# A cleared piece of unused memory behind each row scatter of a routed mixture of experts

## What is computed

```python
x = _layernorm(x + _L0_attn_ref(x, ...))             # gated delta-rule attention, 6 heads
x = _layernorm(x + _L0_xattn_ref(x, ctx, ctx, ...))  # causal softmax attention, 16 heads, 4 of keys
x = _layernorm(x + _L0_ffn_ref(x, ...))              # mixture of experts

# _L0_ffn_ref: 16 routed experts, 2 chosen per token, and 2 shared ones
aff = sigmoid(einsum('bsd,de->bse', x, wa))
topk_p, topk_i = top_k(aff, 2)
topk_p = topk_p / sum(topk_p, axis=-1, keepdims=True)
combine = sum(one_hot(topk_i, 16) * topk_p[..., None], axis=2)
routed = einsum('bsed,bse->bsd', experts_all(x, rg, rgb, rw1, rb1, rw2, rb2), combine)
shared = sum(experts_all(x, sg, sgb, sw1, sb1, sw2, sb2), axis=2)
return x + shared + routed
# an expert: w2(gelu(x g + gb) * (x w1 + b1)) + b2
```

## Time and profile before

| | us |
|---|---|
| median of 3 runs | 576.19 (575.22 to 576.56) |
| the profiled execution | 576.92 |
| its span, first to last instruction | 575.1 |
| TensorE busy | 472.9 (82%) |
| VectorE busy | 364.8 (63%) |
| ScalarE busy | 259.8 (45%) |
| GpSimd busy | 240.9 (42%) |
| L2209, 32 scatters | 31.4 busy, 25.0 idle before them |
| L2231, 48 scatters | 46.2 busy, 61.5 idle before them |

### The profile page before, as it was taken

The page is one execution under the profiler, slowest core; times in us unless marked ns, Lnnn a source line. Parts: engine busy times, 40 slices in busy tenths (PEclk is TensorE's granted clock), DMA queues, the critical chain, the costliest instruction groups (busy, mean ns, idle before and its releaser), DMA issues.

```text
span 575.1 us, 15459 instructions
## 1 busy us (share of the span) xinstructions
PE 472.9 (82%) x5644; PEld 342.5 (60%) x5644; DVE 364.8 (63%) x870; ACT 259.8 (45%) x657; POOL 240.9 (42%) x303
## 2 busy tenths in 40 slices
PE   4969889478769899999689999828983779999765
PEld 2434344244559899997467777614541568888554
DVE  0759468479957566667568799805641067777536
ACT  2557565535663344455366767502100034444316
POOL 0328021246016675643655544170373026555600
PEclk9989999789799999999799999978997979999968
DMA  8980000017662732003660000030053815554284
GB/s 289 284 252 1 0 0 0 2 47 241 237 124 51 181 109 54 22 3 75 249 253 2 3 2 4 6 113 1 30 195 126 284 39 178 163 171 132 84 301 146
DMA packets 62019, 64.00 MB, mean 111 GB/s; under 512 B 31412, under 2 KB 51964, under 8 KB 61564
## 3 DMA queue, kind: packets, MB, share of 16 engines
q1 hardware_dynamic: 58108, 52.29, 29.4%
q0 software_dynamic: 3840, 10.75, 5.2%
HBM read 37.01 MB, written 28.25 MB: 113 GB/s over the span
## 4 chain that ended last, share of the span: by engine, by line
PE 48%; DVE 25%; issue 12%; ACT 5%; SPq 5%; DMA 4%; POOL 1%; DVEq 0%; POOLq 0%; ACTq 0%
PE ps L1161 7%; DVE work L1593 5%; PE ps L732 5%; PE ps L954 4%; DVE work L1772 3%; DVE arena L1776 3%; PE ps L1178 3%; PE ps L722 3%; SPq L675 3%; PE ps L935 2%; PE ps L1083 2%; ACT arena L1440 2%; PE ps L908 2%; PE ps L920 2%; PE ps L886 2%
## 5 line engine op out<-in xcount | busy, mean ns | idle before, releaser
L1593 DVE SCALAR_TENSOR_TENSOR work<-ps,colp,work 96x504 f32<-96x504 f32 (+5 forms) x84 | 59.6, 729 | 21.9 <-ACT work L1235 19.9
L2231 POOL DMA_INDIRECT rows_dr<-work,dest_i x48 | 46.2, 962 | 61.5 <-DVE work L2009 31.2
L1161 PE MATMUL ps<-vsg,work 128*128 x192 | 51.5, 392 | 0.4 <-ACT work L1524 0.4
L732 PE MATMUL ps<-xT,front 128*96 128x512 f32 (+3 forms) x112 | 50.5, 595 | 0.0
L2209 POOL DMA_INDIRECT slots_dr<-xn,slots_i x32 | 31.4, 982 | 25.0 <-issue 9.2
L722 PE MATMUL ps<-front,work 128*128 128x396 f32 x64 | 26.7, 568 | 15.3 <-ACT ab L1228 8.2
L2151 POOL TENSOR_TENSOR arena<-front,consts 128x384 f32<-128x384 f32 x32 | 26.5, 832 | 29.4 <-DMA front<-inverse_dr 24.0
L1530 ACT ACTIVATE work<-work 128x128 f32<-128x128 f32 x48 | 14.8, 309 | 53.0 <-DVE work L1994 43.4
L1994 DVE TENSOR_TENSOR work<-ps,xT 128x256 f32<-128x256 f32 x48 | 20.4, 425 | 28.1 <-PE ps L1161 16.2
L1161 PEld LDWEIGHTS ps<-vsg,work 128*128 128x128 f32 x192 | 33.8, 196 | 3.6 <-issue 0.7
L732 PEld LDWEIGHTS ps<-xT,front 128*96 128x96 f32 (+1 forms) x112 | 19.0, 176 | 26.1 <-issue 25.7
(11 more groups left out here) (247 smaller groups left out, 1236.3 us busy)
## 6 DMA issues: line engine op xcount, KB each, us to landing
work<-slots_dr SPq DMA_DIRECT2D x48, 136.0 KB
vsg<-wexp_dram SPq DMA_DIRECT2D x4, 1536.0 KB, 12.4
vsg<-rows_dr SPq DMA_DIRECT2D x8, 512.0 KB
blocks_dr<-work SPq DMA_DIRECT2D x16, 192.0 KB, 2.5
mats_dr<-work SPq DMA_DIRECT2D x8, 384.0 KB, 3.1
work<-mats_dr SPq DMA_DIRECT2D x3, 768.0 KB, 5.9
slots_dr<-zero SPq DMA_DIRECT2D x8, 272.0 KB
pads_dr<-zero SPq DMA_DIRECT2D x8, 272.0 KB
```

The costliest lines, as they stand in the source:

```text
L732: mm = pe.matmul(ps[0:ROWS[j], BANK[j], :], wc3[:, k, CH0[j]:CH0[j] + ROWS[j]], xT3[:, k, bass.ds(g * GT, GT)], start=(k == 0), stop=(k == ...
L1161: mm = pe.matmul(ps[:, 2 + j % 2, 0:2 * F], xgT[:, j % 2, k, :], wres[:, bass.ds(e + k * 2 * F, 2 * F)], start=(k == 0), stop=(k == KD - 1))
L1593: dve.scalar_tensor_tensor(y[:, :, d:T], z[:, :, 0:T - d], taps[0:r, j, KSZ - 1 - d:KSZ - d], y[:, :, d:T], ALU.mult, ALU.add).then_inc(s_ ...
L2231: pool.indirect_dma_start(out=rows_dr, out_offset=bass.IndirectOffsetOnAxis(ap=dest_i[:, j:j + 1], axis=0), in_=yob[:, j % YO, :], in_offs ...
```

## The change

Behind each scatter of rows GpSimd clears the first 256 columns of `krope`, the rotated keys of the softmax attention, which have no reader by then. Each of these memsets waits for the one before it, through a new counter. There are 32 of them.

```diff
         got = vsg[:, 0:NT * 2 * D].rearrange("p (n k c) -> p n k c", n=NT, k=2)
         ob = vsg[:, NT * 2 * D:NT * 3 * D].rearrange("p (n c) -> p n c", n=NT)
+        pause = krope[:, 0:256]
...
         s_slots = counted("dve", "slots_ready")
+        s_pause = counted("pool", "pauses_between_scatters")
...
                     pool.indirect_dma_start(
                         out=slots_dr, out_offset=bass.IndirectOffsetOnAxis(ap=slots_i[:, c:c + 1], axis=0),
                         in_=xrow[:, n, :], in_offset=None).then_inc(s_scat[b], 16)
+                    if c > 0:
+                        pool.wait_ge(s_pause, at(c))
+                    pool.memset(pause, 0.0).then_inc(s_pause, 1)
```

## The result

The kernel with the change takes 569.99 us (median of 20 runs) where the kernel before, measured beside it, takes 575.5 (20 runs). The ratio is 0.9882 (0.9859 to 0.9906): 6.8 us less, 5.4 to 8.1, where the two medians lie 5.5 apart. Ratios here leave out the executions that lay over 1.5% above the fastest of their kernel. The profiled execution took 567.00 us against 576.92, its span 565.2 against 575.1. On another chip the same change made the kernel slower; that is the larger part of what follows.

The account below looks back on a forecast made before the run. The prediction took closely spaced GpSimd scatters to hold up the other engines in two batches on the chain that ended last. Its terms, -9.7 - 2.5 - 0.5 = -12.7 us, gave 564.0 us, own range 562 to 567, stated range 561.5 to 579.5.

Parts of the forecast that it names:

- three rivals: Whole kernel: rivals 2, 3 and 4, taken in by the stated range of 561.5 to 579.5 us.
- the fetches of q8: Both batches: queue q8's instruction fetches, taken for TensorE's, lie at each stall's head; five in the loop stall nothing.
- Rival 1: Both batches: stalls go by the number of scatters, not their spacing; +8.7 us, 584.9; chance 0.14.
- rival 3: Both batches: spacing stays 1.27 us, or stalls have nothing to do with scatters; no change, 576.2 us; chance 0.08.
- Rival 4: Only the second batch is relieved, the first's fetch coming soon after its first scatter; +2.5 us, 578.7; chance 0.04.
- Price of the pause: Both batches: a memset behind each scatter widens the spacing from 1.27 to 1.57 us, at most 1.94.
- First batch, the stall: End of attention: ScalarE's L1455 no longer waits behind TensorE's ended matmuls of L1029; -9.7 us.
- The clock: After the first stall: TensorE's clock stays up without the idle time; -2.5 us, between 0 and 3.0.
- Second batch: First scatter to SyncE's list reading: memsets cost 5.3 us, SyncE's freedom gives 5.8 back; -0.5 us.
- Rival 2: Only the first batch is relieved, as sixteen large copies run beside the second's scatters; -6.5 us, 569.7; chance 0.08.

Follow-up runs that it names:

- all_late: Kernel before with the first batch's twelve scatters moved behind the clearing and filling of the expert weights, 32 in a row, no pauses; 573.42 us, 0.9990 of before.
- wide_first: Changed kernel with 128x768 memsets in the first batch, the change's own in the second; 563.78 us, 0.9832 of the kernel before, on a chip with stalls.
- fetch_moved: Kernel before plus 120 semaphore additions at the head of TensorE's stream, to shift its instruction fetches; 592.74 us, 1.0334 of before, on a chip with stalls.
- shift_120: Kernel before with 120 empty TensorE instructions that left nothing in the trace, so the kernel before itself; 1.0024 of before, on a chip without stalls.
- wide_only: Kernel before with 128x768 memsets behind the first batch's scatters only, none in the second; 1.0013 of before, on a chip without stalls.
- wide_only_2: Kernel before with 128x768 memsets in the first batch only, run once more on another chip without stalls; 0.9997 of before.
- tiny: Changed kernel with memsets of 128x1 instead of 128x256, waits kept; 0.9999 of the kernel before, on a chip without stalls.
- tiny_again: Changed kernel with 128x1 memsets and their waits, run again on another chip without stalls; 0.9999 of the kernel before.
- second_only: Kernel before with the change's memsets behind the second batch's twenty scatters only; 1.0121 of before, on a chip without stalls.

## Why the prediction was right, and where its size was off

The sum said -12.7 us; the runs say -6.8. The measured 569.99 lies in the stated range, which takes in three rivals, and outside the forecast's own, 562 to 567. All times here are of profiled executions unless a median is named.

**What holds things up.** The prediction read the stalls as the work of closely spaced scatters, and held it against the fetches of q8. On a chip that stalls this is shown: the stall moves with the scatters (all_late), goes with their spacing at an equal number (wide_first), and doesn't mind the fetches (fetch_moved). For all_late this rests on one profiled execution above its median. What sets wide_first apart from the change is the length of the memset; that the same distance without cleared memory would do as well is not shown. Rival 1 (the number) and rival 3 (nothing to do with the scatters) fall. Rival 4 named a fetch soon after the first scatter, which falls too. Not foreseen was that the spacing is one of two conditions. The trace of before was one chip's, and nothing in it could tell that on four others the same kernel takes 556 to 557 us; the one trace that stands for it there, shift_120, has the same spacing.

**Price of the pause.** Forecast 1.57 us from scatter to scatter; 1.46 is usual, 1.53 the mean of the second batch. The memset takes 0.33 instead of 0.303, and the gap in front of a scatter is 0.17 instead of 0.30 when a memset precedes it. That part was good, on the safe side.

**First batch, the stall: -9.7 forecast, -5.6 measured.** This is the step that failed: a distance of 1.57 us was taken to be enough in this batch, and 1.48 was not. It was carried by one comparison: the loop, at 1.61 us, holds nobody up, so 1.57 doesn't either. Twelve scatters at a mean of 1.48 left 4.1 of 9.7 us; at 1.90 they left none (on another chip, but one whose stall, 11.0 us in fetch_moved, is no smaller). The loop's 1.61 us never was evidence for 1.48, and it is not even known to be evidence for 1.57: other engines work beside the loop's scatters than beside these. The second batch, at 1.53, was free all the same. So there is no spacing that could be read off one stage for another; in the first batch it lies somewhere between 1.48 and 1.90.

**The clock: -2.5 forecast, -0.6 measured.** From L1455's start to the second batch it took 413.05 - 385.55 = 27.50 us before and 406.55 - 379.64 = 26.91 after; fetch_moved, whose stall is whole, took 26.88, so even the 0.6 may be none. The lowered clock was expected to go with the idle time. Nearly half the idle time was left, and the clock fell again from 379.5 on: four matmuls of L1044 took 1.72 us at 382.11. In the kernels that didn't stall and had no long pauses the same stretch took 24.8 to 25.0 us, 2.5 to 2.7 less than before, though on other chips. So the term was right for a stall that is gone, and wrong for one that is halved. In wide_first, where the clock stayed up too, it took 403.65 - 377.74 = 25.91, and in wide_only and wide_only_2 25.6 and 26.0: longer pauses take back 0.6 to 1.2 us of it.

**In no term: +1.7.** From the first scatter to the end of the matmuls that ScalarE waits for, before took 375.85 - 371.91 = 3.94 us and after 375.50 - 369.85 = 5.65. The clock stood at 0.50 from 369.2 to 372.6, and L1044 took 1.71 us at 370.65, where L1042 took 0.87 in the trace of before. This is not the change's doing: it set in ahead of the first scatter; fetch_moved, which has no memset, shows the same (0.50 from 390.3 to 393.6, first scatter at 390.48); and one and the same kernel goes either way, tiny with 5.5 us from the first scatter to ScalarE's L1457 and tiny_again with 3.8. The whole stage thus went from 41.14 to 36.70 us: -5.6 - 0.6 + 1.7, or -4.4. In wide_first it is 11.4 us shorter than before, against 12.2 forecast for stall and clock.

**Second batch: -0.5 forecast, -1.2 measured**, from first scatter to first load (33.46 to 32.26 us). The last scatter starts 29.06 us in (forecast 29.8), lands 2.44 later (2.4), and SyncE waits for it and no longer for the copies. The padding copies take 13.7 us of issuing, where 9 to 11 were expected: 0.86 us each, which the scatters cover anyway. VectorE's shared experts are free, as forecast.

**The rest.** The two stages give -4.44 - 1.20 = -5.64, near the -6.8 (5.4 to 8.1) of the medians. The profiled executions lie 9.92 apart. Of what is left, 2.06 stand ahead of the first scatter (369.85 against 371.91), where the kernels are alike, and this start lies anywhere from 368.8 to 373.9 in kernels that don't differ up to there; 1.5 stand between the first load and the loop's first scatter (21.7 against 23.2 us, and 20.9 to 23.5 in the other kernels); 0.7 stand behind it. I count none of them for the change.

**Rival 2** (the first batch relieved, the second not) gave 569.7, a number close to the 569.99 measured, and is wrong all the same: the second batch was relieved in full, the first by over half. That the total came out so near it is luck.

**The sign.** Rival 1 was the only one that ended clearly slower. A slower case did come, on chips 14 and 1, with the price that the prediction had for the pauses of the second batch (19 x 0.30 = 5.7 us forecast, 4.6 measured in that stage) but by a mechanism that it didn't name: no stall to pay for them. The prediction's -0.5 for this batch was a difference of two numbers of 5 to 6 us, one of which depends on the chip. That should have been a rival.

The Trainium skill, "DMA: Bandwidth & Descriptors", section "SWDGE vs HWDGE vs iDMA", was cited for the rule that transfers issued by GpSimd and by SyncE stand in different queues which the DMA engines take in turn. The profile lists them apart, as q0 and q1 (fetch_moved, 434 to 466); the taking of turns itself no run shows. On a chip without stalls, 0.57 of the DMA engines' time is in use from 400 to 427 in shift_120, and TensorE is busy 22.35 of the 27 us beside it: scatters and copies run side by side there and hold nobody up, as by that rule. On chips with stalls the hold-up is in issuing, and in engines that issue no DMA at all, and the rule doesn't reach that.

**What stays open.** What differs between the chips or occasions; by which path scatters hold up ScalarE's, VectorE's and SyncE's start (the profile shows only "remote" and "issue"); whether the waits between the scatters help without the cleared memory; which engine's instructions q14 brings; and how wide_only does where there are stalls. Of the kernels measured beside a stalling one, wide_first is the best (0.9832), better than the change's 0.9882, though on another chip. Two points are argued and not shown: that its second batch would still cost some 5 us on a chip without stalls, as in second_only, and that the longer pauses of the first batch would cost at most about 1 us there, as in wide_only.

## What to carry to other kernels

A pause between scatters belongs where the batch has slack behind it; there it can be made long enough at little cost (none was measurable in wide_only, on chips without stalls), while in a batch that is itself the path it must first earn its own length. When an engine waits long for something that has ended, beside a burst of another engine's work, take the profile again on a second chip before building on it: what is to be removed may not be there. A spacing that is harmless in one stage is a bound for that stage alone.

## What the runs showed of the hardware

**One kernel, two times.** The same kernel before took 574 to 576 us on two occasions and 556 to 557 on four, steadily in each (medians). Between the trace of before and shift_120 the two stages with the stalls account for 18.1 us, as worked out above.

**VectorE and the scatters.** Two scatters of the second batch take 1.71 and 1.49 us. VectorE (first two rows) and GpSimd, kernel after:

```profile
409.43 0.96 DVE L1947 TENSOR_TENSOR arena<-work,consts 128x768 f32<-128x768 f32 x1
411.42 0.96 DVE L1949 TENSOR_TENSOR work<-arena,work 128x768 f32<-128x768 f32 x1
...
409.53 1.71 POOL L2211 DMA_INDIRECT slots_dr<-xn,slots_i  x1 [0.17 <-issue]
411.73 1.49 POOL L2211 DMA_INDIRECT slots_dr<-xn,slots_i  x1 [0.17 <-issue]
```

Both start while VectorE works on two operands, with 0.86 and 0.65 us of it to go, and are longer than 0.97 by 0.74 and 0.52: the remainder less 0.12 or 0.13 each time. second_only and wide_first show the same pair (1.70 and 1.49), and in the kernel before one scatter of the second batch, begun at 418.18 under the same instruction with 0.46 us to go, took 1.30: 0.34 more. A scatter that began under one of the VectorE reductions between them, with one operand (416.91, in the kernel before), took its usual 0.96. The Trainium skill, "SBUF — State Buffer", section "Who interferes with whom", says that a VectorE instruction with two inputs in SBUF gets in the way of a GpSimd instruction that reads SBUF, the later one waiting. The trace agrees where the scatter is the later one. Where it is the earlier one it does not: in the kernel before, VectorE's 128x768 instruction of 415.70, begun 0.05 us behind a scatter, took its usual 0.96, and so did the scatter:

```profile
415.70 0.96 DVE L1945 TENSOR_TENSOR arena<-work,consts 128x768 f32<-128x768 f32 x1
...
415.65 0.96 POOL L2209 DMA_INDIRECT slots_dr<-xn,slots_i  x1 [0.31 <-issue]
```

The Trainium skill also infers there that such an instruction leaves the making of descriptors alone; by these rows a scatter does wait.

**A gap that depends on what went before.** A scatter behind a scatter starts after 0.30 us, one behind a memset after 0.17. A memset of 0.33 us between two scatters so adds only 0.19 to their spacing.

**Additions to a semaphore.** 120 of them on TensorE stand from 5.6 to 23.8 us at the head of fetch_moved, one every 0.153 us:

```profile
L715 PEldq EVENT_SEMAPHORE  x120: 51/51/51, 5.6 to 23.8; - x120
```
